# A Macaron layer on one core: block numbers read one at a time, and denominators laid out by VectorE

## The reference

```python
x = x + 0.5 * ffn(layernorm(x))        # x: 4 batches of 512 tokens, 128 channels
x = x + attention(layernorm(x))
x = x + 0.5 * ffn(layernorm(x))

# ffn: the best 2 of 8 experts for each token, then a layer norm of the mix
logits = (x @ gate_w + gate_b) / 0.9
gate_probs = softmax(top-2 logits)
h = gelu(x @ w1[e] + b1[e])            # 128 -> 512, exact gelu
out = sum over e of gate_probs[e] * (h @ w2[e] + b2[e])

# attention: linear, 16 heads of 64, f(t) = elu(t) + 1
qm, km = f(q), f(k)
kv = einsum('nshd,nshm->nhmd', km, v)
z  = 1.0 / (einsum('nlhd,nhd->nlh', qm, km.sum(axis=1)) + 1e-6)
out = einsum('nlhm,hmf->nlf', einsum('nlhd,nhmd,nlh->nlhm', qm, kv, z), wo) + bo
```

## Time and profile before

| | |
|---|---|
| median of 3 runs | 600.63 us (600.38 to 601.02) |
| profiled execution | 599.01 us, of which the span from first to last instruction is 597.3 us |
| PE busy | 462.7 us, 77% of the span |
| DVE busy | 360.0 us, 60% |
| ACT busy | 286.9 us, 48% |
| POOL busy | 168.6 us, 28% |
| mean granted clock of PE | 0.856 |

### The profile page before, as it was taken

One profiled execution on the slowest core, in us unless ns is written; L12 is line 12 of the kernel. 1 busy time (PEld: TensorE's weight loads), 2 busy tenths in 40 slices (PEclk: granted clock), 3 DMA queues, 4 the chain that ended last, 5 costly groups with the idle time before them and its releaser, 6 DMA issues. The chain is left out here.

```text
span 597.3 us, 8035 instructions
## 1 busy us (share of the span) xinstructions
PE 462.7 (77%) x2559; PEld 346.0 (58%) x2559; DVE 360.0 (60%) x771; ACT 286.9 (48%) x584; POOL 168.6 (28%) x260
## 2 busy tenths in 40 slices
PE   6668798779999919955979698765829999996381
PEld 5546586679985603433545464345319999975260
DVE  4886565589865553564475354242716798656593
ACT  3622884456665721365345340263006766775360
POOL 2584780320004142153020510051600110057610
PEclk7878799899999966987799785885668999998687
DMA  6227743448826800000000000000135767332210
GB/s 155 68 90 259 189 142 124 178 151 291 285 77 236 346 17 19 1 22 14 0 2 1 27 10 0 0 22 14 37 132 177 256 218 247 115 79 66 75 54 18
DMA packets 50816, 62.93 MB, mean 105 GB/s; under 512 B 7771, under 2 KB 36820, under 8 KB 50774
## 3 DMA queue, kind: packets, MB, share of 16 engines
q1 hardware_dynamic: 45892, 53.07, 26.9%
q0 software_dynamic: 3072, 6.30, 3.5%
q10 hardware_dynamic: 1810, 3.04, 1.5%
HBM read 19.84 MB, written 19.43 MB: 66 GB/s over the span
## 5 line engine op out<-in xcount | busy, mean ns | idle before, releaser
L1440 DVE TENSOR_TENSOR hl<-hid,hh 128x1024 fp32r<-128x1024 f32 x70 | 86.6, 1237 | 17.6 <-ACT hh L1164 15.8
L1640 POOL DMA_INDIRECT sorted<-tok,di x48 | 51.6, 1076 | 113.6 <-DVE di L1415 99.8
L1157 ACT ACTIVATE hid<-psA,cols 128x512 f32<-128x512 f32 (+1 forms) x128 | 66.8, 580 | 32.8 <-PE psA L786 24.2
L784 PE MATMUL psB<-hh,W 128*128 128x512 f32 (+1 forms) x128 | 49.7, 388 | 17.7 <-DVE hl L1440 17.7
L1620 POOL TENSOR_SCALAR ve<-mv 128x4 f32<-128x4 f32 x20 | 7.5, 377 | 146.2 <-DVE mv L1269 145.6
L1180 ACT ACTIVATE X<-psA,less 128x1024 f32<-128x1024 f32 x16 | 17.8, 1115 | 60.5 <-PE psA L976 60.5
L786 PE MATMUL psB<-hh,W 128*128 128x512 f32 (+1 forms) x128 | 46.4, 363 | 0.0
L785 PE MATMUL psB<-hl,W 128*128 128x512 f32 (+1 forms) x128 | 46.2, 361 | 0.0
L1655 POOL DMA_INDIRECT g<-results,di x24 | 26.3, 1097 | 62.3 <-DMA results<-yb 55.0
L1189 ACT ACTIVATE X<-psA,cols 128x512 f32<-128x512 f32 x32 | 22.0, 687 | 44.2 <-PE psA L786 44.2
L1043 PE MATMUL psC<-qm,Gs 128*128 128x512 f32 x64 | 41.8, 791 | 1.4 <-DVE qm L1566 1.4
(11 more groups left out here) (253 smaller groups left out, 1266.7 us busy)
## 6 DMA issues: line engine op xcount, KB each, us to landing
Wd<-W SPq DMA_DIRECT2D x44, 512.0 KB, 3.3
sorted<-tok SPq DMA_DIRECT2D x1, 7552.0 KB, 24.5
xb<-sorted SPq DMA_DIRECT2D x38, 128.0 KB, 2.9
results<-yb SPq DMA_DIRECT2D x38, 128.0 KB, 3.1
pb<-gate_table SPq DMA_DIRECT2D x16, 256.0 KB, 3.5
stage<-in_L_ffn_w_dram SPq DMA_DIRECT2D x14, 256.0 KB, 4.8
sorted<-wvT ACTq DMA_DIRECT2D x1, 2432.0 KB, 8.4
out_dram<-x SPq DMA_DIRECT2D x4, 256.0 KB, 2.3
```

The source lines that it names most:

```text
L784: nc.tensor.matmul(o, ah, bh, start=start, stop=False)
L1157: last = nc.scalar.activation(hid[:, u % 2, q * width:(q + 1) * width], ps(st)[:, q * width:(q + 1) * width], ACT.Gelu, bias=bias)
L1440: nc.vector.tensor_tensor(hl[:, u % HS, :], hid[:, u % 2, :], hh[:, u % HS, :].bitcast(F32), ALU.subtract)\
L1640: nc.gpsimd.indirect_dma_start(xs[ix(r)], bass.IndirectOffsetOnAxis(di[:, ix(r), k, j:j + 1], 0), tok[:, j, :], None)\
```

## The change

SP no longer reads all numbers at the beginning. `expert_of` and `rows_of` read a number when the first DMA that needs it is issued, and the loads at the first sparse block are put in another order. The denominators are written twice next to each other (`ksum` gets four small copies, so that rows 0 to 15 and 16 to 31 of every 32 hold the same 16 heads), and DVE writes them, as four 32x128 instructions, on the diagonal of a 128x512 array `zq`, in which the lower half of each 32 rows holds the low part. PE reads `zq` directly, with a `pick` of 128 rows. The constants for this are made on DVE in a step `picks`; `prep` moves from POOL to DVE at the same place of the list; POOL writes fewer constants. Several kinds of steps get names of their own at the same place in the list (`split`).

```diff
+            def expert_of(r, k):
+                if (r, k) not in expert:
+                    expert[r, k] = sp.value_load(tab[0:1, ix(r), 0, k - E:k - E + 1], min_val=0, max_val=E - 1)
+                return expert[r, k]
...
-                return xs[1][bass.ds(row[k - E], BW), :]
+                if k not in row:
+                    row[k] = sp.value_load(tab[0:1, 1, 1, k - E:k - E + 1], min_val=0, max_val=ROWS2 - BW)
+                return xs[1][bass.ds(row[k], BW), :]
...
+                        load_xb(u)
                         sp.wait_ge(tab_ready, ix(r) + 1)
-                        for i in range(DYN):
-                            expert[r, i] = sp.value_load(tab[0:1, ix(r), 0, i:i + 1], min_val=0, max_val=E - 1)
-                            if r == FFN2:
-                                row[i] = sp.value_load(tab[0:1, 1, 1, i:i + 1], min_val=0, max_val=ROWS2 - BW)
-                        for v in first:
-                            load_wd1(v)
-                        for v in range(u, u + 4):
-                            load_xb(v)
-                        for v in first:
-                            load_wd2(v)
+                        load_wd1(first[0])
+                        load_xb(u + 1)
+                        load_wd1(first[1])
+                        load_xb(u + 2)
+                        load_xb(u + 3)
+                        load_wd2(first[0])
+                        load_wd2(first[1])
...
-                        last = nc.scalar.copy(ksum[hs, j:j + 34 * HP - 33:34], ksum_ps[hs, :])
+                        for d in (0, 16):
+                            last = nc.scalar.copy(ksum[hs, d + j:d + j + 34 * HP - 33:34], ksum_ps[hs, :])
...
-                elif kind == "denz" and a[1] == 1:
-                    n = a[0]
-                    act.wait_ge(z_split, n + 1)
...
-                    for q in range(4):
-                        for k in range(2):
-                            last = nc.scalar.copy(z2[32 * k:32 * k + 16, q * P:(q + 1) * P],
-                                                  zhl[32 * q:32 * q + 16, k, :].bitcast(F32))
...
-                    link(nc.vector.tensor_copy(zhl[:, 0, :], zr))
-                    nc.vector.tensor_tensor(zhl[:, 1, :], zr, zhl[:, 0, :].bitcast(F32), ALU.subtract).then_inc(z_split, 1)
+                    link(nc.vector.tensor_copy(zh[:, :], zr))
+                    for t in range(ST):
+                        q = slice(32 * t, 32 * (t + 1))
+                        last = nc.vector.scalar_tensor_tensor(zq[q, t * P:(t + 1) * P], zh[q, :].bitcast(F32), lower[q, 0:1], zr[q, :],
+                                                              ALU.mult, ALU.add)
+                    last.then_inc(z_ready, 1)
...
+                elif kind == "prep":
...
+                    link(nc.vector.memset(kt0[:, :, :], 0.0))
+                    for hs in (slice(0, 64), slice(64, P)):
+                        nc.vector.tensor_copy(kt0[hs, :, hs], cols[hs, 48:56].unsqueeze(2).to_broadcast([64, HP, 64])).then_inc(prep_ready, 1)
+                elif kind == "picks":
+                    nc.vector.tensor_reduce(head, ident[:, :].rearrange("p (b h) -> p h b", h=2 * HP), AX_X, ALU.add)
+                    link(nc.vector.tensor_reduce(lower[:, :], ident[:, :].rearrange("p (b l h) -> p l b h", l=2, h=2 * HP)[:, 1, :, :],
+                                                 AX_XY, ALU.add))
+                    nc.vector.tensor_scalar(lower[:, :], lower[:, :], -1.0, None, ALU.mult)
+                    nc.vector.tensor_copy(pick[:, :, :].rearrange("p c (j m) -> p (c j) m", j=2),
+                                          head.unsqueeze(2).to_broadcast([P, 2 * HP, P // 2])).then_inc(pick_ready, 1)
```

More of the change, by code:

```diff
@@ L20 @@
 AX_X = mybir.AxisListType.X
+AX_XY = mybir.AxisListType.XY
 P = 128
@@ L210, in timeline, with split @@
     t += [("accT", FFN2, "C"), ("fstat", FFN2, 3), ("finish", FFN2, 3), ("store", 3)]
-    return t
+    return split(t)
+def split(t):
+    out = []
+    for st in t:
+        kind, a = st[0], st[1:]
+        if kind == "comb":
+            out.append(("top1", *a))
+        if kind == "denz":
+            if a[1] == 0:
+                out.append(("denz", a[0]))
+            continue
+        out.append(st)
+        if kind == "z":
+            out.append(("qz", *a))
+        elif kind == "xT":
+            out.append(("xl", *a[:2]))
+        elif kind == "oT":
+            out.append(("att", *a))
+        elif kind == "gate":
+            out.append(("logits", *a[:2]))
+        elif kind == "Kf" and a[1] > 0:
+            out.append(("kt", *a))
+        elif kind == "consts":
+            out.append(("picks",))
+    return out
 def bass_macaron_kernel(nc: bass.Bass, x_in, wq, bq, wk, bk, wv, bv, wo, bo, gate_w, gate_b,
@@ L268, in bass_macaron_kernel @@
         wo2 = g[:, :, :, :].rearrange("p a t m -> p (a t m)").rearrange("p (c m) -> p c m", c=HP)
-        pick = sb("pick", [48, HP, P], F32R)
-        z2 = sb("z2", [48, BANK], F32R)
+        pick = sb("pick", [P, HP, P], F32R)
+        zq = sb("zq", [P, BANK], F32R)
+        lower = sb("lower", [P, 1])
         ksum = sb("ksum", [P, HP * 32])
@@ L322, in bass_macaron_kernel @@
         cuts = le[:, 0:E, :]
+        head = le[:, 0:2, :].rearrange("p a e -> p (a e)")
         ek = sb("ek", [P, DYN])
@@ L524, in xT_step, with gate_step @@
             return next(st for st in steps if st[0] == "xT" and st[1:3] == (r, n))
+        def gate_step(r, n):
+            return next(st for st in steps if st[0] == "gate" and st[1:3] == (r, n))
         def accT_step(r):
@@ L1028, in _ @@
                     n, j = a
+                    pe.wait_ge(pick_ready, 1)
                     pe.wait_ge(z_ready, n + 1)
@@ L1031, in _ @@
                         c = 2 * j + q
-                        last = nc.tensor.matmul(ps(st)[:, q * BANK:(q + 1) * BANK], pick[:, c, :], z2[:, :], start=True, stop=True)
+                        last = nc.tensor.matmul(ps(st)[:, q * BANK:(q + 1) * BANK], pick[:, c, :], zq[:, :], start=True, stop=True)
                     last.then_inc(full["A"], 1)
@@ L1119, in _ @@
                             wait_full(act, ("Q", 2, 3))
+                            wait_full(act, ("K", 2, 3))
                         nc.scalar.copy(xh[:, xslot(r, n), :], ps(st)[:, 0:BT]).then_inc(xh_ready, 1)
                     if r != ATT:
-                        earlier = [s2 for s2 in steps[:at[st]] if s2[0] == "gate"]
-                        if earlier:
-                            wait_full(act, earlier[-1])
+                        if xg_count[st] > 1:
+                            wait_full(act, gate_step(*next(s2[1:3] for s2 in xg_count if xg_count[s2] == xg_count[st] - 1 and s2[1] != ATT)))
+                        if r == FFN2:
+                            act.wait_ge(x_final, place[("finish", FFN1, DENSE[FFN1])] + 1)
                         nc.scalar.copy(xg[:, :], ps(st)[:, 0:BT]).then_inc(xg_ready, 1)
@@ L1328, in _ @@
                     if i == 0:
-                        dve.wait_ge(logits_read, sum(s2[0] == "gate" for s2 in steps[:at[st]]))
+                        dve.wait_ge(logits_read, max(place[gate_step(r, n)] for n in GROUPS[r][gi]) + 1)
                         dve.wait_ge(route_consts, 1)
@@ L1494, in _ @@
                     dve.wait_ge(stats_ready, s + 1)
+                    if is_dense(r, n):
+                        for m in range(NB):
+                            wait_full(dve, gate_step(r, m))
                     dve.wait_ge(ln_loaded, 32)
@@ L1537, in _ @@
                         .then_inc(feature_ready, 1)
[L1538 to L1550 removed]
+                elif kind == "kt":
+                    n, i = a
+                    dve.wait_ge(feature_ready, feature_use[("K", n, i)] + 1)
+                    ktf = kt[:, :, :].rearrange("p c m -> p (c m)")
+                    if i > 1:
+                        dve.wait_ge(kt_added, (ST - 1) * n + i - 1)
+                    elif n == 0:
+                        dve.wait_ge(down_done, U_END1)
+                    else:
+                        dve.wait_ge(ksum_full, n)
+                    first = km[:, (ST * n) % 2, :] if i == 1 else ktf
+                    nc.vector.tensor_tensor(ktf, first, km[:, (ST * n + i) % 2, :], ALU.add).then_inc(kt_added, 1)
+                elif kind == "prep":
+                    dve.wait_ge(cols_ready, 1)
+                    dve.wait_ge(consts_ready, 1)
+                    link(nc.vector.memset(kt0[:, :, :], 0.0))
+                    for hs in (slice(0, 64), slice(64, P)):
+                        nc.vector.tensor_copy(kt0[hs, :, hs], cols[hs, 48:56].unsqueeze(2).to_broadcast([64, HP, 64])).then_inc(prep_ready, 1)
+                elif kind == "picks":
+                    dve.wait_ge(ident_ready, 1)
+                    nc.vector.tensor_reduce(head, ident[:, :].rearrange("p (b h) -> p h b", h=2 * HP), AX_X, ALU.add)
[4 more added lines that the diff above has]
```

(3 more changed lines are left out.)

94 lines of the change are left out of this document (34 added, 60 removed).

## The result

The changed kernel takes 577.8 us (median of 4, 576.7 to 579.4) beside 600.8 for the kernel before: ratio 0.961, interval 0.957 to 0.965, so 23 us faster. The forecast was 594.4, with a range of 589 to 599. The direction was right, the size was not: 23 us came off, where 6.2 had been forecast.

The account below looks back on a forecast made before the run. No engine's total bounds the kernel, but a chain over many lines, with waits at FFN2's start, batch 0's denominators and FFN1. Terms +2.0 - 2.5 + 1.2 + 0.5 + 1.2 - 9.1 + 0.5 = -6.2 gave 594.4 us, range 589.0 to 599.0.

Parts of the forecast that it names:

- direct cost of the denominators: Attention, per batch: two more `ksum` copies on ACT, +0.34 us; four DVE instructions replacing one, +0.85; PE's column counts stay.
- Start of FFN2: FFN2's beginning: SP's reads hold up PE; reordering gains 9.1 us, reads moved into the stream cost +0.5.
- Batch 0: Attention's first batch: ACT's eight copies go, `z` comes earlier, the layer norm is the next wait; gain 2.5 us.
- Batches 1 to 3: Attention's later batches: PE did not wait for the removed copies; added ACT and DVE work costs +2.9 us.
- FFN1: Dense part of FFN1: `prep` on DVE delays `acc` and the weights ACT awaits, +2.0 us.
- The cover of `picks`: FFN1: `picks` on DVE costs nothing, covered by room gained as POOL's constants go; without that, up to +1.3 us.
- the removal of the early reads in FFN1: FFN1: eleven early SP reads lay ahead of a stage waiting for other things; taken as no gain.
- More is gained: Rival, chance 0.20: 589 to 592 us; PE's clock stays higher at FFN2's start (-1.3), or FFN1's 2.0 also hides.
- The reads hold SP up: Rival, chance 0.08: reads in the stream delay SP's queue; 601 us and up, 609.6 if all 15.7 reach PE.
- a sign that the prediction had named as wrong: Sparse stage: PE waiting for `Wd` or rows in mid-stage, where no such wait existed, would show the forecast wrong.

Follow-up runs that it names:

- a_prep_pool: The changed kernel with the step prep (a clear and two copies) back on GpSimd instead of VectorE: 576.2 us, ratio 0.956 to the kernel before.

## Why the prediction was wrong

By ratios, step by step from kernel to kernel, with 600.8 us as the measure: both products at 128 rows 1.000 to 0.964, 21.7 us faster; the denominators' layout 0.964 to 0.969, 3.4 slower; the reads 0.969 to 0.956 (a_prep_pool), 7.8 faster; prep on VectorE 0.956 to 0.961, 2.8 slower. The sum is the measured 23, as it must be when each step begins where the one before ends. Each interval reaches some 2 us to either side, so the two steps that cost, of about 3 us, are known in sign rather than size.

**The step that failed** stands in the direct cost of the denominators: "The high part's conversion, the inverse and PE's column counts stay." That is true, and from it I concluded that PE's products cost the same; the K bias, which the change widened too, had no term at all. So PE's own work was put at nothing, while the rows alone, with nothing else changed, took 21.6 of the 23 us. A product of 48 rows among products of 128 holds PE up, and the wider arrays took that away. The kernel before showed it, at the rows at 178.35 to 179.44 above, and I had not looked at PE's starts there, since the column count was equal and no wait was marked: PE is shown as busy throughout.

The rows' direct worth is 32 x 0.388 = 12.4 for the K bias. For the denominators, a pair of products and the starts on both sides took 0.99 at one full-speed place of before (307.43 to 308.42) and 0.69 after (297.97 to 298.66), so with 16 pairs up to 4.8. That is 17 of 21.6.

The rest is in the clock. Over the attention the granted clock was 0.81 before, in 258.5 us, and 0.86 with rows alone, in 235.6; with levels of 0.5 and 1 that is an estimated 98 and 66 us at the lower one. I compared every start of PE in the attention between these two traces. Where PE had no wait and the same level in both, rows alone is 13.4 shorter; where the levels differ, 15.3 (the rows' saving there included); and its waits are 5.7 longer, which together makes the 22.9. One place shows it by itself. PE's timeline before:

```profile
368.39 3.78 PE L1043 MATMUL psC<-qm,Gs 128*128 128x512 f32 x4
371.96 2.83 PE L995 MATMUL psB<-km,xn 128*128 128x512 f32 x4
```

And with rows alone:

```profile
350.30 1.88 PE L1043 MATMUL psC<-qm,Gs 128*128 128x512 f32 x4
352.01 1.88 PE L995 MATMUL psB<-km,xn 128*128 128x512 f32 x4
```

These eight products have 128 rows in both kernels and PE does not wait, yet up to the next product they take 6.33 at a granted clock of 0.57 before and 3.03 at 1.00 with rows alone.

**What stays open** is why the clock rose, and how much of it the rows brought about. The kernel before with only the reads moved has the old rows and 0.81 over its attention, and yet it ran these eight products at 1.00, in 3.64; so of the 3.3 us above, 2.7 are the clock and 0.6 the rows of the products on either side. Raising the clock by added products in batch 0 gave nothing in time. And the runs of one kernel differ by 2 to 9 us.

**Start of FFN2: the mechanism was right, the size too large.** The forecast was -9.1 + 0.5 = -8.6. Against reads at the front in the same kernel the stages show -7.7 + 1.4 = -6.3 and the times only -1.4 (ratios) or -3.1 (medians); the two other pairs of kernels show -7.6 and -7.8. Three choices were off. The last scatter landed late: I took the median 2.2 where the largest, 3.3, is what a wait for all of them sees (the earlier trace rows has both), so SP's first load came 419.53 - 416.18 = 3.35 after the last scatter's issue. PE ended the attention sooner after that issue than before, 420.15 - 416.18 = 3.97 in place of 435.75 - 430.46 = 5.29, so more of the loads showed as a wait. And I priced the register load of every read at the 0.27 that it takes behind another read; in the stream, the median read of a row number took 0.88 (below). PE's two waits, 1.70 and 3.27, had been forecast at about 1 and some 2.

**Batch 0: right.** Forecast -2.5, and the layer norm next; between the two layouts the transposes moved by -2.0, and the wait for the layer norm is there.

**Batches 1 to 3: the mechanism was right, the size a little small.** Forecast +2.9. Between the two layouts the traces go from 2.0 ahead in batch 0 to 1.6 behind at the counts and 2.1 behind at the last output (411.54 against 409.40), so +3.6 to +4.1; by the times it is some +5. DVE's four instructions cost 1.25 each time rather than 0.85: I took the price of a row with 128 partitions, where four took 1.14, but these take 1.42. The `ksum` copies cost less than forecast: four take 0.47 where two took 0.35.

**FFN1: right for prep, with a term put at nothing that was not.** Forecast +2.0; 2.26 at `acc`, 2.2 at ACT's weights, +2.3 at the first K product. The cover of `picks` was as said: `hl` takes 1.22 where it took 2.17, and the routing matrix reaches PE 2.4 earlier. But the changed kernel's trace is the latest of five with the same FFN1 (173.8 to 175.7, above). For the removal of the early reads in FFN1 I took nothing; with prep on GpSimd, the median of the first K product is 172.8 with the reads in the stream and 173.7 in the six kernels with the reads at the front, so it gives back about 1.

**The rivals.** "More is gained" is what happened in size, though not by its mechanism. FFN1 was not hidden, and at FFN2's start the clock fell all the same, to 0.50 from 424.8 to 428.2 in the trace after; that is 3.4 us where it had been 6.4, so a part of this rival's 1.3 to 2.7 at most. The higher clock that counted was in the attention. "The reads hold SP up" is there at 1.4 to 2.6 us (the rest of the span in the pairs of traces that differ by the reads), far from its price of 15.7. PE has two new waits of about 1 us in the sparse stage after, the second of them a sign that the prediction had named as wrong:

```profile
PE psB L822 <- ACT yb L1212: 1.4, 1, 1.4
PE psC L899 <- DMA xb<-sorted: 0.9, 1, 0.9
```

The larger one is a stored result, as the rival had it. ACT could write `yb` again only when SP's store had left it, and that store was issued at 482.15, behind two reads, a load of rows and two of weights. ACT's timeline:

```profile
486.96 0.37 ACT L1212 COPY yb<-psB 128x256 f32<-128x256 f32 x1 [2.94 <-DMA results<-yb]
```

## What to carry to other kernels

When an edit changes a product's shape, read the distance between the starts of the products around it, not the durations or the waits: an engine can lose time where the trace shows it busy. Here it paid to pad a small contraction between full ones to 96 or 128 rows, which were equal, rather than leave it at 48 or 64. Count each such product: 0.39 us, 32 times over, were worth more than the change gained at either of the waits that it was made for. And a part that rides along in a change may be its whole gain, while the part it is named for costs: price each alone before keeping all.

## What the runs showed of the hardware that was not expected

- A product with 48 or 64 rows between products with 128 (512 columns each) costs 0.39 us of PE's time at a granted clock of 1.00, the same for both, spread over three starts: its own, the next one's and the one after that. At 96 rows it costs nothing. At 0.50 it was 0.59: the three starts were 0.56, 0.72 and 0.59 apart at 284.69 before, and 0.43 each with 128 rows.
- Reading a number from SBUF into a register of SP takes 0.27 us in the median behind another read, also with scatters in flight, and mostly 0.84 to 0.90 right behind the issue of a load of weights or a bias, or of a store. That weights are in flight is not enough: right behind a load of rows it took 0.27 at 479.47, while weights issued at 476.50 were landing until 479.61. Row numbers (L682) and expert numbers (L687, each behind a load of rows) in FFN2's sparse part after, 430 to 490 us:

```profile
L682 SPq TENSOR_LOAD <-tab x9: 533/882/904, 429.7 to 477.7; - x9
L687 SPq TENSOR_LOAD <-tab x9: 263/390/845, 432.0 to 479.5; - x9
```

- Four VectorE instructions of 32x128 take longer in a row (1.42) than four of 128x128 of the same operation (1.14). One alone takes the same in both, 0.34. They differ in more than the shape (the 32x128 ones write fp32r, each to other partitions), and which of these makes them overlap less was not tried.
